# A recurrence of 64 steps: the transposition of the weights is moved from behind the state products to behind their sixth round of eight, in some of the steps

## The chip, the cores and the metric

The kernel runs on one core of a Trainium2 chip. The metric is the device time of one execution in microseconds (us). Before the change it was 16686.17 us, the median of three runs (16681.96 to 16693.16).

## The reference

The program is a whole audio tower of four layers. The change touches one part of it: the recurrent fast-weight layer in the third layer's attention, which is, for each of 64 positions `t` of a sequence and for all frames and heads (cut to what matters):

```python
def rec_step(carry, inp):
    R, h = carry
    zt, kt, vt, bt = inp
    qh = jax.nn.softmax(h, axis=-1)
    v_old = jnp.einsum('bhij,bhj->bhi', R, kt)
    R = R + (bt * (vt - v_old))[..., :, None] * kt[..., None, :]
    h = zt + jnp.einsum('bhij,bhj->bhi', R, qh)
    return ((R, h), h)
_, hs = jax.lax.scan(rec_step, (R0, h0), (z, rk, rv, rbeta))
```

An earlier stage of the kernel has already turned the updates of `R` into rows `ur`, so that `R` at step t is a sum of products of a row of `ur` and a key of `kr`. What is left for each step is `h = z + R softmax(h)`, for 246 independent states of 64 x 64 at a time. All is float32.

## The kernel before, in words

`recur_stage` runs eight passes (four pairs of heads, two halves of the frames), each of `SL = 64` steps. A pass keeps its states in two groups, a = 0 and a = 1, of 124 and 122 rows (frame and head on the partitions). The 64 steps are four quarters of `SC = 16` steps. The state matrices `R` hold what came before the current quarter; what came within the quarter is taken from its keys `K` and rows `U` directly. A step t with n = t mod 16 + 1 does, for a group:

- ScalarE: `e = exp(h - max)` with its sum (L2881).
- VectorE, `dots`: `pr = K * e` over n keys (L3000), its sum `dot` (L3005), then `w = dot * par8`, which spreads each dot over eight columns (L3009), then two small operations for the division by the sum. From t = 16 on, VectorE does `finish` of the other group between L3005 and L3009.
- TensorE, `turn`: transposes `w` into PSUM, as `wT` (L2921), one instruction.
- ScalarE, `spread`: copies `wT` to `W`, in the places that the next products read (L2868).
- TensorE, `turn_exp`: turns `e` into PSUM, as `eT` (L2927, two products, four MATMULs in the trace, since a float32 product is two). ScalarE, `spread_exp`, copies it to `E` (L2876, two copies). It serves the state products of the step's own `e`.
- TensorE, `state`: the product of `R` with `E`, eight rounds of four products of 32 columns each (L2939, 64 MATMULs), summed in the bank `acc[a]`.
- TensorE, `recent`: the product of `U` with `W` on top of it (L2948, 16 products, 32 MATMULs). Its last one tells VectorE.
- VectorE, `finish`: adds to the row of `H` (L3026 twice), and takes its maximum (L3027), which lets ScalarE do the next exp.

In the first quarter `R` is zero, and there are no state products. In the first three quarters the next quarter's state is prepared beside the steps: TensorE multiplies a sixteenth of it per step (`make_state`, L2964), ScalarE copies it to `made` (`take_state`, L2889), and GpSimd adds it to the old state, `R_new = made + R_old` (L2859, in the second and third quarter, 16 per quarter; in the first it copies, L2861).

There is no scheduler: each engine's order is written out by hand in its block, and the engines wait for each other by semaphores. The order of TensorE from step 16 on, which the change touches, is: state(0, t), turn(0, t), turn_exp(1, t), recent(0, t), make_state, state(1, t), turn(1, t), turn_exp(0, t + 1), recent(1, t). `turn` waits for `s_dot` (L3009 done), `recent` for `s_dg` (L2868 done). ScalarE's order from step 16 on is exp of group 1, spread(0, t), spread_exp(1, t), exp of group 0, spread(1, t), spread_exp(0, t + 1), take_state(t).

Of the kernel before, what the change touches and what calls it, by code (L numbers as in the profile page):

```python
# [441 lines left out]
SC = 8  # L442
# [2242 lines left out]
def recur_stage(nc, c, kr, ur, zz, hs):  # L2685


    SC, NL = 16, 4
# [5 lines left out]
    with Stage(nc, "recur") as st:  # L2694
# [91 lines left out]
        def run(i, half, following):  # L2786
            with st.step() as block:
# [128 lines left out]
                @block.tensor  # L2916
                def _(pe):
                    def turn(a, t):
                        n = t % SC + 1
                        pe.wait_ge(s_dot[a], t + 1)  # L2920
                        nc.tensor.transpose(wT[a][0:8 * n, 0:128], w[a][:, 0:n, :].rearrange("p s k -> p (s k)"), c.ident[:]).then_inc(s_tr[a], 1)  # L2921

                    def turn_exp(a, t):
                        cp = 2 * GROUPS[a][1]
                        pe.wait_ge(s_ex[a], t)
                        for h in range(2):
                            ins = nc.tensor.matmul(eT[a][64 * h:64 * h + 64, 0:128], e[a][0:cp, :], Ih[0:cp, h, :], start=True, stop=True)  # L2927
                        ins.then_inc(s_et[a], 1)

                    def state(a, t):  # L2930
                        rows = R[t // SC % 2][:].rearrange("p (a y) m d -> p a (y m) d", a=2)[:, a]
                        if t % SC == 0:
                            pe.wait_ge(s_rk, NMK * (t // SC))
                        pe.wait_ge(s_eg[a], 2 * (t - SC + 1))
                        for j in range(8):
                            u, v = divmod(j, 4)
                            for q in range(4):
                                m = 16 * q + 8 * u + v
                                nc.tensor.matmul(acc[a][32 * q:32 * q + 32, 0:2 * FD].rearrange("p (w d) -> p w d", w=2),  # L2939
                                                 E[a][:, EQ * q + 32 * j:EQ * q + 32 * j + 32], rows[:, m:m + 5:4, :], start=(j == 0), stop=False)  # L2940

                    def recent(a, t):
                        n = t % SC + 1
                        pe.wait_ge(s_dg[a], t + 1)
                        for j in range(4):
                            at = FD * (j % 2) if t >= SC else 0
                            for q in range(4):
                                ins = nc.tensor.matmul(acc[a][32 * q:32 * q + 32, at:at + FD], W[a][0:8 * n, 160 * q + 32 * j:160 * q + 32 * j + 32],  # L2948
                                                       U[a][0:8 * n, t // SC % 2, 4 * q + j, :], start=(t < SC and j == 0), stop=(j == 3))
                        ins.then_inc(s_sum[a], 1)  # L2950

                    def make_state(k, n):
                        b = NB * k + n // 4
                        pe.wait_ge(s_rin[b % 2], 16 * 12 * (b // 2 + 1))
                        if NMK * k + n:
                            pe.wait_ge(s_rc, 2 * (NMK * k + n))
                        a = n % 2
                        for x in range(4):
                            m = 4 * (n // 2) + x
                            for y in range(2):  # L2960
                                if 32 * y + m < GROUPS[a][1]:
                                    rows = slice(64 * a + 32 * y, 64 * a + 32 * y + SC)
                                    for h in range(2):
                                        ins = nc.tensor.matmul(Rp[y][64 * h:64 * h + 64, x, :], Ks[b % 2][rows, m % PB, h, :], Us[b % 2][rows, m % PB, h, :], start=True, stop=True)  # L2964
                        ins.then_inc(s_rm, 1)

                    for t in range(SL):
                        if t and t % SC == 0:
                            pe.wait_ge(s_in[t // SC], 16 * 24)
                        if t < SC:  # L2970
                            for a in range(2):
                                turn(a, t)
                                recent(a, t)
                                if t >= SC - NMK // 2:
                                    make_state(0, 2 * (t - (SC - NMK // 2)) + a)
                            if t == SC - 1:
                                turn_exp(0, SC)
                        else:
                            state(0, t)
                            turn(0, t)  # L2980
                            turn_exp(1, t)
                            recent(0, t)
                            if t < SL - SC:
                                make_state(t // SC, t % SC)
                            state(1, t)
                            turn(1, t)
                            if t + 1 < SL:
                                turn_exp(0, t + 1)
                            recent(1, t)
# [1237 lines left out]
```

## Time and profile before

| | |
|---|---|
| median of three runs | 16686.17 us |
| the profiled execution's own time | 16682.81 us |
| its span, from first to last instruction | 16681.0 us |
| granted clock of TensorE over the span | 0.824 of full |
| recurrence: from the first transposition of `w` to the last `finish` | from 9947.1 to 13578.8 us of the span |
| TensorE busy over the span | 12670.9 us (76%) |
| VectorE busy over the span | 9806.6 us (59%) |
| ScalarE busy over the span | 6771.4 us (41%) |
| state products, L2939, 49152 MATMULs | 1559.1 us busy |
| recent products, L2948, 32768 MATMULs | 785.7 us busy |
| transpositions of `w`, L2921, 1024 | 342.0 us busy |

TensorE's MATMULs are pipelined: their modelled ends reach past the start of the next ones, so a busy share near 100% doesn't mean that it has no pauses. Starts are what can be read. PE is TensorE's matmul, PEld its weight load, DVE VectorE, ACT ScalarE, POOL GpSimd. One step takes some 6 to 8 us, and there are 48 steps with state products in each of eight passes.

### The profile page before, as it was taken

What the parts mean: (1) busy time and instruction counts of PE and PEld (TensorE: products, weight loads), DVE (VectorE), ACT (ScalarE), POOL (GpSimd) and SP (SyncE); (2) the same over time, 40 slices, a digit from 0 to 9 for tenths busy, and PEclk for the clock granted to TensorE, in tenths of its full rate; (3) what the DMA queues carried; (4) which work ended last, traced back from release to release, by engine and by line L of the source; (5) the groups of instructions that cost most, each with busy time, mean ns of one, the idle gap of its engine ahead of it and who ended that gap; (6) DMA issues with size and microseconds to landing.
All of it is one profiled execution on the core that took longest, in us unless ns stands there. A gap on an engine that the chain in (4) does not pass through costs nothing. (4 is left out here: it accounts for less than half of the span.)

```text
span 16681.0 us, 559673 instructions
## 1 busy us (share of the span) xinstructions
PE 12670.9 (76%) x241781; PEld 9937.0 (60%) x241781; DVE 9806.6 (59%) x25450; ACT 6771.4 (41%) x17683; POOL 2665.7 (16%) x1778
## 2 busy tenths in 40 slices
PE   5605677886186498898999978988888885868887
PEld 4503475665154377777777757766666674745655
DVE  6561247776411566666666657777777755437885
ACT  3100125663021366666666643333333331336651
POOL 0028501000447011111111111111111100000001
PEclk9555558886586699999999988888888896968986
DMA  0412321003133211111111112122222244159862
GB/s 22 115 24 47 81 46 37 21 22 84 38 74 50 83 27 26 27 27 26 27 27 26 27 37 56 47 56 53 52 55 53 50 128 123 39 168 257 251 180 68
DMA packets 1829102, 1109.34 MB, mean 67 GB/s; under 512 B 1097198, under 2 KB 1751441, under 8 KB 1808657
## 3 DMA queue, kind: packets, MB, share of 16 engines
q1 hardware_dynamic: 1599239, 1015.52, 24.4%
q0 software_dynamic: 227328, 57.19, 2.4%
q8 instruction: 1936, 31.72, 0.8%
q14 instruction: 599, 4.91, 0.1%
HBM read 585.55 MB, written 484.53 MB: 64 GB/s over the span
## 5 line engine op out<-in xcount | busy, mean ns | idle before, releaser
L2939 PE MATMUL recur_acc<-recur_R,recur_E 128*32 128x128 f32 x49152 | 1559.1, 279 | 44.6 <-POOL recur_R L2859 27.8
L2939 PEld LDWEIGHTS recur_acc<-recur_R,recur_E 128*32 128x32 f32 x49152 | 1341.9, 112 | 107.3 <-issue 62.5
L2475 ACT ACTIVATE delta_B1l<-delta_pS 64x256 f32<-64x256 f32 x1968 | 743.6, 378 | 709.3 <-PE delta_pS L2375 683.6
L2475 ACT ACTIVATE delta_B0l<-delta_pS 64x256 f32<-64x256 f32 x1968 | 743.5, 378 | 623.4 <-PE delta_pS L2375 602.6
L3000 DVE TENSOR_TENSOR recur_pr<-recur_K,recur_e 124x64 f32<-124x64 f32 (+31 forms) x1024 | 751.1, 734 | 218.1 <-ACT recur_e L2881 171.8
L2510 POOL TENSOR_TENSOR delta_QK<-delta_QK,delta_mx 128x512 f32<-128x512 f32 x369 | 379.7, 1043 | 3044.4 <-DVE delta_mx L2563 3044.4
L2948 PE MATMUL recur_acc<-recur_U,recur_W 8*32 8x64 f32 (+1 forms) x32768 | 785.7, 244 | 105.2 <-ACT recur_W L2868 95.5
L2948 PEld LDWEIGHTS recur_acc<-recur_U,recur_W 8*32 8x32 f32 (+1 forms) x32768 | 596.9, 123 | 355.1 <-ACT recur_W L2868 346.9
L2868 ACT ACTIVATE recur_W<-recur_wT 8x128 f32<-8x128 f32 (+15 forms) x1024 | 278.1, 272 | 1277.1 <-PE recur_wT L2921 1260.3
L2881 ACT ACTIVATE recur_e<-recur_H,recur_mx 124x64 f32<-124x64 f32 x1008 | 350.8, 348 | 1056.9 <-DVE recur_mx L3027 1056.6
L3005 DVE TENSOR_REDUCE recur_dot<-recur_pr 124x1 f32<-124x64 f32 (+31 forms) x1024 | 736.8, 719 | 34.1
L3026 DVE SCALAR_TENSOR_TENSOR recur_H<-recur_acc,recur_rm,recur_H 124x64 f32<-124x64 f32 (+1 forms) x1536 | 435.8, 284 | 534.1 <-PE recur_acc L2948 493.8
L2375 PE MATMUL delta_pM<-delta_B1l 64*64 64x128 f32 (+1 forms) x11808 | 740.1, 256 | 5.3 <-ACT delta_B1l L2478 4.3
L2375 PE MATMUL delta_gp<-delta_W,delta_xc 128*128 128x512 f32 x1230 | 699.3, 653 | 37.2 <-DVE delta_xc L2546 37.0
L2375 PE MATMUL delta_pM<-delta_B0l 64*64 64x128 f32 (+1 forms) x11808 | 716.5, 255 | 4.8 <-ACT delta_B0l L2478 3.6
L2375 PE MATMUL delta_gp<-delta_KT 64*64 64x64 f32 x11808 | 563.0, 224 | 183.2 <-ACT delta_KT L2497 143.3
L2375 PEld LDWEIGHTS delta_pM<-delta_B1l 64*64 64x64 f32 x11808 | 600.2, 133 | 100.4 <-issue 89.1
L2375 PEld LDWEIGHTS delta_pM<-delta_B0l 64*64 64x64 f32 x11808 | 581.7, 133 | 126.0 <-ACT delta_B0l L2478 98.8
L1207 POOL DMA_INDIRECT hB<-experts_y,experts_idx x256 | 619.1, 2418 | 101.2 <-issue 80.8
L2525 DVE TENSOR_TENSOR delta_B1l<-delta_B1l,delta_pM 128x256 f32<-128x256 f32 x738 | 310.7, 421 | 545.1 <-PE delta_pS L2375 545.1
L2921 PE MATMUL recur_wT<-const_ident,recur_w 128*8 128x128 f32 (+15 forms) x1024 | 342.0, 334 | 374.3 <-DVE recur_w L3009 368.6
L2375 PE MATMUL delta_pM<-delta_B 64*64 64x128 f32 x7872 | 536.7, 275 | 101.4 <-issue 86.4
(626 smaller groups left out, 34033.6 us busy)
## 6 DMA issues: line engine op xcount, KB each, us to landing
scr<-rel_BD SPq DMA_DIRECT2D x128, 1288.0 KB
rel_sc<-scr SPq DMA_DIRECT2D x128, 861.0 KB
xnT<-ln_xT SPq DMA_DIRECT2D x64, 492.0 KB, 3.0
kr<-delta_QK SPq DMA_DIRECT2D x492, 64.0 KB, 2.3
ur<-delta_Uf SPq DMA_DIRECT2D x492, 64.0 KB, 2.2
zz<-delta_Z SPq DMA_DIRECT2D x492, 64.0 KB, 2.2
recur_K<-kr SPq DMA_DIRECT2D x64, 448.0 KB
recur_H<-zz SPq DMA_DIRECT2D x64, 448.0 KB
```

The lines of the kernel that those rows point to most:

```text
L1207: nc.gpsimd.indirect_dma_start(acc[:, :], bass.IndirectOffsetOnAxis(ap=idx[:, e, 4 * q + t:4 * q + t + 1], axis=0), y[n % 3][:, t, :], Non ...
L2375: return nc.tensor.matmul(o, l, r, start=True, stop=True)
L2475: ins = nc.scalar.activation(new[h, :, 0, :], pS[k][HALF[1 - x], 0:4, :], ACT.Copy)
L2510: nc.gpsimd.tensor_tensor(third(j), third(j), mx[:, rows_of(j)].unsqueeze(2).to_broadcast([128, FH, FD]), ALU.subtract).then_inc(s_sh, 1)
L2525: V.tensor_tensor(level(k, G % 2, l + 1)[:, :, 2, :], u, pM[k][:, :, 1, :], ALU.subtract if l == 0 else ALU.add).then_inc(s_dv[k], 1)
L2881: nc.scalar.activation(e[a][0:cp], Hh[a][0:cp, t, :], ACT.Exp, bias=mx[a][0:cp, 0:1], accum_out=rs[a][0:cp, 0:1]).then_inc(s_ex[a], 1)
L2921: nc.tensor.transpose(wT[a][0:8 * n, 0:128], w[a][:, 0:n, :].rearrange("p s k -> p (s k)"), c.ident[:]).then_inc(s_tr[a], 1)
L2939: nc.tensor.matmul(acc[a][32 * q:32 * q + 32, 0:2 * FD].rearrange("p (w d) -> p w d", w=2), E[a][:, EQ * q + 32 * j:EQ * q + 32 * j + 32], ...
L2948: ins = nc.tensor.matmul(acc[a][32 * q:32 * q + 32, at:at + FD], W[a][0:8 * n, 160 * q + 32 * j:160 * q + 32 * j + 32], U[a][0:8 * n, t // ...
L3000: V.tensor_tensor(pr[0:cp, 0:n, :], K[a][0:cp, r0:r0 + n, :], e[a][0:cp, None, :].to_broadcast([cp, n, FD]), ALU.mult).then_inc(s_own[a], 1)
L3005: own[a](V.tensor_reduce(dot[a][0:cp, 0:n], pr[0:cp, 0:n, :], AX.X, ALU.add))
L3026: own[a](V.scalar_tensor_tensor(row, acc[a][0:cp, FD * z:FD * z + FD], rm[a][0:cp, z:z + 1], row, ALU.mult, ALU.add))
```

## The change

In the first eight steps of a quarter (t mod 16 < 8), `turn(a, t)` is issued inside `state(a, t)`, behind its sixth round. In the other steps it is issued right behind the state products, as before. The first quarter has no state products, and its order is as it was.

```diff
                     def state(a, t):
+                        soon = t % SC < 8
                         rows = R[t // SC % 2][:].rearrange("p (a y) m d -> p a (y m) d", a=2)[:, a]
                         if t % SC == 0:
                             pe.wait_ge(s_rk, NMK * (t // SC))
                         pe.wait_ge(s_eg[a], 2 * (t - SC + 1))
                         for j in range(8):
+                            if soon and j == 6:
+                                turn(a, t)
                             u, v = divmod(j, 4)
                             for q in range(4):
                                 m = 16 * q + 8 * u + v
                                 nc.tensor.matmul(acc[a][32 * q:32 * q + 32, 0:2 * FD].rearrange("p (w d) -> p w d", w=2),
                                                  E[a][:, EQ * q + 32 * j:EQ * q + 32 * j + 32], rows[:, m:m + 5:4, :], start=(j == 0), stop=False)
+                        if not soon:
+                            turn(a, t)
...
                         else:
                             state(0, t)
-                            turn(0, t)
                             turn_exp(1, t)
                             recent(0, t)
                             if t < SL - SC:
                                 make_state(t // SC, t % SC)
                             state(1, t)
-                            turn(1, t)
                             if t + 1 < SL:
                                 turn_exp(0, t + 1)
                             recent(1, t)
```

So 8 steps x 3 quarters x 8 passes x 2 groups = 384 of the 768 transpositions behind state products move. No instruction is added or taken away, and the orders of VectorE, ScalarE, GpSimd and the DMA queue stay as they were.

TensorE in the second quarter, steps 17 and 18 of a pass, before (each row is a run of equal instructions: `recur_acc<-recur_R` are the state products, `recur_wT` the moved transposition, `recur_eT` the turned exp, `recur_acc<-recur_U` the recent products, `recur_Rp` the next state):

```order
L2939 MATMUL recur_acc<-recur_R,recur_E 32x128 x32
L2921 MATMUL recur_wT<-const_ident,recur_w 16x128
L2927 MATMUL recur_eT<-recur_Ih,recur_e 64x128 x2
L2948 MATMUL recur_acc<-recur_U,recur_W 32x64 x16
L2964 MATMUL recur_Rp<-recur_Us,recur_Ks 64x64 x16
L2939 MATMUL recur_acc<-recur_R,recur_E 32x128 x32
L2921 MATMUL recur_wT<-const_ident,recur_w 16x128
L2927 MATMUL recur_eT<-recur_Ih,recur_e 64x128 x2
L2948 MATMUL recur_acc<-recur_U,recur_W 32x64 x16
```

The same place with the change:

```order
L2942 MATMUL recur_acc<-recur_R,recur_E 32x128 x24
L2921 MATMUL recur_wT<-const_ident,recur_w 16x128
L2942 MATMUL recur_acc<-recur_R,recur_E 32x128 x8
L2927 MATMUL recur_eT<-recur_Ih,recur_e 64x128 x2
L2953 MATMUL recur_acc<-recur_U,recur_W 32x64 x16
L2969 MATMUL recur_Rp<-recur_Us,recur_Ks 64x64 x16
L2942 MATMUL recur_acc<-recur_R,recur_E 32x128 x24
L2921 MATMUL recur_wT<-const_ident,recur_w 16x128
L2942 MATMUL recur_acc<-recur_R,recur_E 32x128 x8
L2927 MATMUL recur_eT<-recur_Ih,recur_e 64x128 x2
L2953 MATMUL recur_acc<-recur_U,recur_W 32x64 x16
```

The transposition now stands eight products (16 MATMULs) earlier, and the turned exp follows the last two rounds in its place.

## Rows read from the trace of the kernel before

**Rows 1.** Who waited for whom, whole recurrence: us in total, times, longest.
```profile
PEld recur_acc L2948 <- ACT recur_W L2868: 346.9, 1024, 0.7
...
PEld recur_acc L2939 <- issue: 62.5, 63, 2.0
```
**Rows 2.** Timeline of TensorE, second quarter, step 20: start us, us, instruction, xcount.
```profile
10533.98 1.95 PE L2939 MATMUL recur_acc<-recur_R,recur_E 128*32 128x128 f32 x64
10535.86 0.29 PE L2921 MATMUL recur_wT<-const_ident,recur_w 128*40 128x128 f32 x1
...
10536.51 0.65 PE L2948 MATMUL recur_acc<-recur_U,recur_W 40*32 40x64 f32 x32
...
10537.71 1.95 PE L2939 MATMUL recur_acc<-recur_R,recur_E 128*32 128x128 f32 x64
10539.60 0.29 PE L2921 MATMUL recur_wT<-const_ident,recur_w 128*40 128x128 f32 x1
10539.82 0.44 PE L2927 MATMUL recur_eT<-recur_Ih,recur_e 124*64 124x128 f32 x4
...
10540.83 0.86 PE L2939 MATMUL recur_acc<-recur_R,recur_E 128*32 128x128 f32 x24
```
**Rows 3.** TensorE's weight loads, same step; in brackets idle time before, and its releaser.
```profile
10536.51 0.49 PEld L2948 LDWEIGHTS recur_acc<-recur_U,recur_W 40*32 40x32 f32 x32 [0.23 <-ACT recur_W L2868]
...
10539.60 0.10 PEld L2921 LDWEIGHTS recur_wT<-const_ident,recur_w 128*40 128x40 f32 x1 [0.20 <-issue]
```
**Rows 4.** Timeline of the other engines, same step.
```profile
10534.43 1.28 POOL L2859 TENSOR_TENSOR recur_R<-recur_made,recur_R 128x512 f32<-128x512 f32 x1 [6.16 <-ACT recur_made L2889]
...
10534.94 0.82 DVE L3009 TENSOR_TENSOR recur_w<-recur_dot,recur_par 124x40 f32<-124x40 f32 x1
...
10540.52 0.67 ACT L2889 ACTIVATE recur_made<-recur_Rp 128x256 f32<-128x256 f32 x2
...
10541.27 1.28 POOL L2859 TENSOR_TENSOR recur_R<-recur_made,recur_R 128x512 f32<-128x512 f32 x1 [5.56 <-ACT recur_made L2889]
```
**Rows 5.** Timeline of TensorE, fourth quarter, step 50, group 0.
```profile
10751.41 1.96 PE L2939 MATMUL recur_acc<-recur_R,recur_E 128*32 128x128 f32 x64
10753.30 0.28 PE L2921 MATMUL recur_wT<-const_ident,recur_w 128*24 128x128 f32 x1
10753.51 0.44 PE L2927 MATMUL recur_eT<-recur_Ih,recur_e 122*64 122x128 f32 x4
10753.93 0.65 PE L2948 MATMUL recur_acc<-recur_U,recur_W 24*32 24x64 f32 x32
10754.51 1.95 PE L2939 MATMUL recur_acc<-recur_R,recur_E 128*32 128x128 f32 x64
```
**Rows 6.** Timeline of VectorE, the same half-step.
```profile
10752.38 0.17 DVE L3009 TENSOR_TENSOR recur_w<-recur_dot,recur_par 124x24 f32<-124x24 f32 x1
```
**Rows 7.** Groups of instructions by form, recurrence: count, busy us, mean ns, idle before.
```profile
L2859 POOL TENSOR_TENSOR recur_R<-recur_made,recur_R 128x512 f32<-128x512 f32 x256 | 327.6, 1280 | 1578.1 <-ACT recur_made L2889 1578.1
```
**Rows 8.** Timeline of TensorE, fourth quarter, steps 57 and 59.
```profile
10794.33 0.65 PE L2948 MATMUL recur_acc<-recur_U,recur_W 72*32 72x64 f32 x32
10794.80 1.93 PE L2939 MATMUL recur_acc<-recur_R,recur_E 128*32 128x128 f32 x64
...
10809.43 0.44 PE L2927 MATMUL recur_eT<-recur_Ih,recur_e 122*64 122x128 f32 x4
10809.80 0.66 PE L2948 MATMUL recur_acc<-recur_U,recur_W 96*32 96x64 f32 x32
```
**Rows 9.** Timeline of TensorE in a later stage: transpositions, then products of the same shape.
```profile
13604.75 0.58 PE L3115 MATMUL dout_tp<-const_ident,dout_t 123*128 123x123 f32 x4
13605.18 1.04 PE L3124 MATMUL dout_yp<-dout_wo,dout_tT 128*123 128x128 f32 x8
```
**Rows 10.** Timeline of TensorE, third quarter, step 33 of the fourth pass.
```profile
11539.32 0.49 PE L2948 MATMUL recur_acc<-recur_U,recur_W 16*32 16x64 f32 x18 [1.45 <-issue]
```
**Rows 11.** Busy us (x count) of PE, PEld, DVE, ACT, POOL; granted clock; DMA share, GB/s.
```profile
11551.79:11556.37 4.58, 4.58 (x103) 3.55 (x101) 0.45 (x1) 0.73 (x4) 0.00 (x0) 0.63 0.26 63
```

## The prediction

> **What bounds the kernel now.** I read four views, for the recurrence alone, since nothing outside it changes. First the waits: they say what TensorE stands for. The largest that the change aims at is the recent products' wait for ScalarE's copy of the transposed weights, 346.9 us over 1024 times [rows 1]. Then the timelines of one step in the second quarter [rows 2 to 4] and one in the fourth [rows 5, 6], because the step, not the total, tells what a wait is worth. All offsets below are counted from the start of a state product, S.
>
> In step 50 nothing interrupts TensorE: S, transposition at 1.89, turned exp at 2.10, recent products at 2.52, next S at 3.10 [rows 5]. TensorE bounds these steps; VectorE's multiply by `par8`, which the transposition needs, runs from 0.97 to 1.14 and is long ready [rows 5, 6]. In step 20, group 1, the times are the same: 1.89 to the transposition, 2.11 to the turned exp, 3.12 to the next S [rows 2]. Group 0 has `make_state` behind it, 3.73 to the next S, and one difference that the TensorE rows don't show: its multiply starts at 0.96 and lasts 0.82 instead of 0.17, to 1.78. GpSimd's addition runs from 0.45 to 1.73, and the multiply ends 0.05 after it [rows 4, 6]. I read this as the multiply being held by the addition. Today that costs nothing: at 1.78 TensorE is just through with the state products, and the transposition comes at 1.88 [rows 2].
>
> The reader is also to see the pauses around the transposition. The weight load before it idles 0.20 with "issue" as its releaser, so it waits for nobody [rows 3]. It is a change of shape: state products (32 columns, four side by side), transposition (whole columns), turned exp (64 columns). Two checks: recent products of 24 rows take 0.58 to the next S, those of 72 rows 0.47 [rows 5, 8], although both are followed by the same semaphore wait, so the 0.11 goes with the shape and not with the wait; and four transpositions followed by products of like shape take 0.43, that is 0.107 each, with no pause [rows 9].
>
> **The change, part by part.** The eight rounds take 1.89 - 0.20 = 1.69 up to the pause [rows 3, 5], 0.21 each; at a steady pace, with 0.107 to 0.109 for 128 columns [rows 9] and two passes a round, 0.22. Two rounds are 0.44.
>
> Moved, a free half-step. The transposition comes at 1.89 - 0.44 = 1.45. Its multiply must be ready by then: 1.14 in the fourth quarter, and earlier in group 1 of the middle quarters. So it doesn't wait. From it to the seventh round I take 0.205, as from the transposition to the turned exp today (0.21 [rows 5]); nearest below is 0.107 [rows 9], without a change of shape. The seventh round starts at 1.655, its last MATMUL 0.375 later (16 MATMULs are four groups 0.109 apart, and a start after a pause costs 0.025 once) at 2.03, and the turned exp 0.205 behind it at 2.24, against 2.10: later by **0.14**. The split adds one more change of shape.
>
> Removed: the wait for ScalarE's copy. The copy now ends well before. The turned exp to recent products can shrink from 0.43 to 0.37, its value in step 59 [rows 8], for its own four MATMULs and a change of shape remain. So recent products start at 2.61 against 2.52, and a free half-step gets longer by **0.08**. Bounds: with 0.107 out of the transposition it is -0.02; with no gain at the recent products +0.14. I take the middle value, since the rows show this very pair of shapes in the other order [rows 3, 5].
>
> Moved, a held half-step: group 0 where the addition runs. GpSimd's addition follows ScalarE's copy of `made`, which stands behind the two copies of the turned exp. It starts 10541.27 - 10539.82 = 1.45 after group 1's turned exp [rows 2, 4]. From there to the next S it is now 1.01, and then 0.37 + 0.44 + 0.14 = 0.95. So the addition starts at 0.50 and ends at 1.78, the multiply ends at 1.84, and the transposition starts at 1.90, where TensorE wanted it at 1.45: **TensorE stands 0.45**, with two state rounds, the other group's turned exp and the recent products queued behind it. Then 2.10 seventh round, 2.48 its last, 2.69 turned exp, 3.06 recent products, against 2.53: longer by **0.53**. Today the same lateness lies under rounds seven and eight. VectorE behind it has room: what it does between the held multiply and its next `finish` is short at up to eight keys; if that cover were gone, the lateness would be added once more, which I price at nothing.
>
> Counts. Additions: 256, 32 per pass, 16 in each middle quarter [rows 7]. The addition of step t holds the multiply of step t + 1, so of the first eight steps of those two quarters seven are held, 14 per pass, 112 in all (the eighth begins a quarter, where S waits for the addition before). Free are 384 - 112 = 272.
>
> Sum: 112 x 0.53 = 59, 272 x 0.08 = 22, together 81. Cover: TensorE also stands for "issue" in the middle of uniform runs, 1.45 us in one of them [rows 10], 62.5 us over 63 times before state products alone [rows 1]. No data is late there; I read it as late instructions. Where such a stall falls before round seven the hold is over, and a slower TensorE asks for its instructions a little later; I take off 4, about an eighth of the part of these stalls that could lie in the first halves. So **+77 us**. The profiled execution's own time, 16682.81, lies 3.4 below the median, 16686.17; from the median it is 16763.
>
> **A rule of the Trainium skill against the rows.** The load of the transposition's weights idles 0.20 behind the last state MATMUL while its operand is ready [rows 3]. The Trainium skill, "TensorE: Matmul & The Clock Gate", Part 2 and Part 3, says that TensorE's queue pulls weight loads ahead of running MATMULs when their row groups don't conflict or when they go to the background weights. By that a transposition could slip between two rounds with no pause. The trace doesn't agree for this pair of shapes. What the sum would be without the pauses is rival 1.
>
> **Rivals.**
> 1. *The split costs no pause.* Transposition 0.107 after round six and round seven 0.107 after it. For it: the transpositions that need no pause [rows 9]. Against: the idle load [rows 3]. A free half-step: 1.35 transposition, 1.46, 1.81 last MATMUL, 2.02 turned exp, 2.39 recent: -0.13, together -35; a held one still waits to 1.90, 2.01, 2.36, 2.57, 2.94: +0.41, together +46. Sum +11: 16697, no change. 6%.
> 2. *Faster: no pause, and no hold.* One mechanism, that of rival 1, in all 384 places: it needs the addition out of the way. ScalarE's copy of the weights of group 1 comes 0.44 earlier, and if that, not the turned exp, sets when `made` is copied, the addition ends before 1.40. Price -0.13 x 384 = -50: 16636. It decides when the addition ends before 1.40. Against it: the copies of the turned exp stand between and need TensorE. 5%.
> 3. *The cover is larger.* If late instructions hide half of the sum: +40, 16726. 12%.
> 4. *The clock falls as well.* A state product at granted clock 0.63 took 4.58 for its half-step instead of 3.1 [rows 11], so 1.5 more. TensorE now stands 0.45 in seven successive steps. Against: even behind a stop of 1.45 the next products ran at full pace [rows 10]. One fall per middle quarter is 16 x 1.5 = +24: 16787; one in each held step would be 112 x 1.5 = +168: 16931. 7%.
>
> **How the numbers follow.** My forecast, hold and pause both there, has 70%: 16763, between 16725 (pauses at their low bound, 43) and 16795 (no gain at the recent products, 38 + 66 = 104). About 0.2%, 33 us, is what a measurement can tell from no change. Slower than 16719: the forecast 69%, rival 3 9% (its low side falls within), rival 4 7%: 0.85. Within: rival 1 5% and what is left of the forecast and rival 3: 0.09. Faster: 0.06, rival 2 and a rest. The range of 8 in 10 takes in rival 3, the bounds, and one fall of the clock per quarter: 16712 to 16805.
>
> **What would show it.** In the profile after: in free half-steps, state MATMULs in two runs, 48 and 16, with pauses of 0.20 on both sides of the transposition, turned exp at 2.24, recent products at 2.61, next S at 3.18. The recent products' wait for ScalarE gone in 384 of 1024 places. In held ones the transposition at 1.90 with an idle TensorE before it and VectorE's `recur_w` as its releaser, next S at 4.26. It would be wrong if the seventh round followed the transposition by 0.11, or if the multiply ended before 1.45 in group 0 of steps 17 to 23.

## The result, and the profile after

The changed kernel took 16729.48 us, median of 19 runs (16701.87 to 16752.46); the kernel before, beside it, 16685.37 us (19 runs, 16662.25 to 16703.78). The ratio is 1.0026, with a 95% interval of 1.0020 to 1.0032: **slower by 44 us**, 33 to 53. The forecast was +77 us, 16763, with a range of 16712 to 16805. The sign and the mechanisms held; the measured cost is 33 us smaller than the forecast.

The profiled execution has a span of 16724.3 us, 43.3 more than before. All of it lies in the recurrence: its eight passes take 3541.2 us before and 3584.4 after, each counted from its first transposition of `w` to its last recent product, +43.2.

TensorE in step 20 of the second pass, as in [rows 2] (columns as there):

```profile
10541.61 1.52 PE L2942 MATMUL recur_acc<-recur_R,recur_E 128*32 128x128 f32 x48
10543.50 0.29 PE L2921 MATMUL recur_wT<-const_ident,recur_w 128*40 128x128 f32 x1 [0.38 <-DVE recur_w L3012]
10543.72 0.64 PE L2942 MATMUL recur_acc<-recur_R,recur_E 128*32 128x128 f32 x16
10544.30 0.44 PE L2927 MATMUL recur_eT<-recur_Ih,recur_e 122*64 122x128 f32 x4
10544.67 0.65 PE L2953 MATMUL recur_acc<-recur_U,recur_W 40*32 40x64 f32 x32
...
10545.87 1.52 PE L2942 MATMUL recur_acc<-recur_R,recur_E 128*32 128x128 f32 x48
10547.32 0.29 PE L2921 MATMUL recur_wT<-const_ident,recur_w 128*40 128x128 f32 x1
10547.54 0.64 PE L2942 MATMUL recur_acc<-recur_R,recur_E 128*32 128x128 f32 x16
10548.11 0.44 PE L2927 MATMUL recur_eT<-recur_Ih,recur_e 124*64 124x128 f32 x4
10548.48 0.65 PE L2953 MATMUL recur_acc<-recur_U,recur_W 40*32 40x64 f32 x32
10549.06 0.64 PE L2942 MATMUL recur_acc<-recur_R,recur_E 128*32 128x128 f32 x16
```

Group 1, the free half-step, reads 1.45 to the transposition, 2.24 to the turned exp, 2.61 to the recent products and 3.19 to the next state product, where the prediction had 1.45, 2.24, 2.61 and 3.18. Group 0, the held one, reads 1.89, 2.69, 3.06 and 4.26, where it had 1.90, 2.69, 3.06 and 4.26. The weight loads of group 0's half-step, and GpSimd's and VectorE's rows of it, as in [rows 3, 4]:

```profile
10543.50 0.10 PEld L2921 LDWEIGHTS recur_wT<-const_ident,recur_w 128*40 128x40 f32 x1 [0.64 <-DVE recur_w L3012]
...
10544.30 0.20 PEld L2927 LDWEIGHTS recur_eT<-recur_Ih,recur_e 122*64 122x64 f32 x4 [0.20 <-issue]
10544.66 0.49 PEld L2953 LDWEIGHTS recur_acc<-recur_U,recur_W 40*32 40x32 f32 x32 [0.17 <-issue]
```
```profile
10542.12 1.28 POOL L2859 TENSOR_TENSOR recur_R<-recur_made,recur_R 128x512 f32<-128x512 f32 x1 [6.15 <-ACT recur_made L2889]
```
```profile
10542.58 0.87 DVE L3012 TENSOR_TENSOR recur_w<-recur_dot,recur_par 124x40 f32<-124x40 f32 x1
```

The load before the recent products no longer names ScalarE's copy, as it did in [rows 3]: what is left there, 0.17, is the change of shape. The load before the transposition now idles 0.64 for the multiply, which ends 0.05 behind GpSimd's addition. The waits of the whole recurrence, as in [rows 1]:

```profile
PEld recur_acc L2953 <- ACT recur_W L2868: 256.5, 640, 0.7
...
PEld recur_acc L2942 <- issue: 58.9, 75, 2.0
```

640 places are left of 1024, so the wait for the copy went in exactly the 384 that moved, and 90 us of waiting with it. The kernel is slower all the same, because 384 new pauses and 112 held transpositions stand in their place.

The steps cost what the sum said. Their medians give 0.53 to 0.54 for a held half-step and 0.08 for a free one, so 112 x 0.535 + 272 x 0.08 = 82 us. The passes got only 43 longer. So 39 us of the cost are hidden somewhere, where the prediction took off 4 (39 us is 82 - 43). The experiments ask two things: whether the two terms are what they were taken for, and what hides 39 us.

### The profile page after: what moved, and what is told of

Read it like the earlier page. It is cut to its first block and busy times, and to the rows that moved or that the text cites. A ratio compares the mean times of both kernels' runs of the same rounds, so it can differ in the third digit from the quotient of the medians.

```text
span 16724.3 us, 559673 instructions
## 1 busy us (share of the span) xinstructions
PE 12682.6 (76%) x241781; PEld 9898.1 (59%) x241781; DVE 9824.3 (59%) x25450; ACT 6778.9 (41%) x17683; POOL 2668.4 (16%) x1778
## 5 line engine op out<-in xcount | busy, mean ns | idle before, releaser
L2942 PE MATMUL recur_acc<-recur_R,recur_E 128*32 128x128 f32 x49152 | 1623.6, 279 | 40.8 <-POOL recur_R L2859 27.9
L2942 PEld LDWEIGHTS recur_acc<-recur_R,recur_E 128*32 128x32 f32 x49152 | 1304.9, 111 | 147.4 <-issue 58.9
```

## Experiments: the terms of the sum

Theory: the pauses and the hold cost what the steps show, and what hides part of it are TensorE's stalls for late instructions, with the clock falls behind them (a fall: a stretch in which the granted clock is 0.5 of full, the level of 1.2 GHz). Rivals: the hold is the whole cost; or both terms are too large by the same factor. The kernel before, measured beside these four, took 16662.85 us (30 runs).

**Only the free places.**

```diff
-                        soon = t % SC < 8
+                        soon = t % SC < 8 and (a == 1 or t % SC == 0 or t >= SL - SC)
```

> The transposition moves only where GpSimd's addition doesn't hold the multiply: group 1 in the first eight steps of a quarter, both groups in step 0 of a quarter and in the fourth quarter, 272 places. Theory (the step times of the prediction are right, and what was missing of its sum was stalls for late instructions and falls of the clock, which shrink only where TensorE is held back long): +0.08 us each, +22 us in all, stalls in the second and third quarter as before. Rival 1 (the pauses around the transposition cost nothing in sum, the whole +44 comes from the hold): 0 us. Rival 2 (both parts of the sum are too large by the same factor, 44/81): +12 us.

Measured: 16679.78 us, ratio 1.0008 (0.9999 to 1.0017), +13 us with an interval of -2 to +28. The time alone excludes neither +22 nor +12, nor quite 0. The steps decide against the rival that the pauses are free: behind the first step of a quarter, the moved half-steps at full clock read 3.18 to 3.20 in place of 3.10 to 3.13.

**Only the held places.**

```diff
-                        soon = t % SC < 8
+                        soon = 0 < t % SC < 8 and a == 0 and t < SL - SC
```

> The transposition moves only in the 112 held places: group 0, steps 1 to 7 of the second and third quarter. Theory: the seven half-steps get 0.53 us longer each, 59 us in all, and the stalls for late instructions with the clock falls behind them give back some 35: +24 us. Rival 1 (the whole cost is the hold): +44 us. Rival 2 (same factor): +32 us. The half-step of group 0 should read 4.26 in place of 3.73 in all three, so the difference lies in what is idle for late instructions and in the granted clock.

Measured: 16705.15 us, ratio 1.0026 (1.0015 to 1.0036), +43 us, 25 to 60. The expected half-step of 4.26 was a slip of mine: group 1 keeps its old order here, so the addition starts at 0.45 and not at 0.50, and the half-step reads 4.21.

```profile
10536.69 1.52 PE L2942 MATMUL recur_acc<-recur_R,recur_E 128*32 128x128 f32 x48
10538.53 0.29 PE L2921 MATMUL recur_wT<-const_ident,recur_w 128*40 128x128 f32 x1 [0.32 <-DVE recur_w L3012]
...
10540.90 0.32 PE L2942 MATMUL recur_acc<-recur_R,recur_E 128*32 128x128 f32 x4
```

That is +0.47, 52 us over 112. The time is that of the first rival, and the theory's +24 lies just outside the interval. The rival's reason, free pauses, is refuted by the steps of the run above; what the time does show is that the hold is most of the cost, and that I set the cover too high for this kernel: 52 by the steps against 43.

**Behind the seventh round.**

```diff
-                            if soon and j == 6:
+                            if soon and j == 7:
```

> As the change, but the transposition stands behind the seventh round in all 384 places. Free places: the same three changes of shape, +0.08 each, the transposition at 1.67 in place of 1.45, next S still 3.18. Held places: the multiply still ends at 1.84, one state round less is queued behind it: next S at 4.05 in place of 4.26, +0.31 each. Sum of the steps 22 + 35 = 57 against 81 for the change; theory with a cover of some 25 to 35: +25 us, rival (the hold is all, the pauses nothing): 112 x 0.23 = +26 us with the free places at 3.10. The profile tells the two apart, not the time.

Measured: 16696.54 us, ratio 1.0024 (1.0015 to 1.0033), +40 us, 25 to 55. In the profile the free half-steps read 3.18, the held ones 4.05:

```profile
10516.86 1.74 PE L2942 MATMUL recur_acc<-recur_R,recur_E 128*32 128x128 f32 x56
10518.76 0.29 PE L2921 MATMUL recur_wT<-const_ident,recur_w 128*40 128x128 f32 x1 [0.16 <-DVE recur_w L3012]
...
10520.91 0.32 PE L2942 MATMUL recur_acc<-recur_R,recur_E 128*32 128x128 f32 x4
```

Both are the theory's numbers. The transposition is no later than behind round six, 1.90, but one round less is queued behind it. The time is less good for the theory: it said +25, after a cover of 25 to 35 us, and +40 is more, though still within the interval. By the steps alone it would be +57.

**The hold taken away.** ScalarE's copy of the next state goes ahead of its exp of group 0, so that GpSimd adds in group 1's half-step:

```diff
                             spread_exp(1, t)
+                            if t < SL - SC:
+                                take_state(t)
                             if t + 1 < SL:
                                 exped(0, t)
...
-                        if SC <= t < SL - SC:
-                            take_state(t)
```

> The changed kernel, with ScalarE's copy of the next state moved ahead of its exp of group 0, in place of behind the copies of the turned exp. GpSimd's addition then runs in group 1's half-step, before the multiply of group 0 is due. Theory (the multiply is held by the addition): the multiply of group 0 in steps 1 to 7 lasts 0.17 to 0.2 us again and the half-step 3.81 in place of 4.26, all 384 places are free: +31 us from the step times, little cover, and perhaps some 10 us less since steps 8 to 13 no longer wait for it either. Rival (the multiply is late for another reason, and only ends with the addition by chance): it still ends at 1.84, and the time is that of the change, +44 us.

Measured: 16677.97 us, ratio 1.0009 (1.0000 to 1.0018), +15 us. The multiply lasts 0.19 again, and the transposition comes at 1.45 in group 0 as well:

```profile
10518.55 1.52 PE L2942 MATMUL recur_acc<-recur_R,recur_E 128*32 128x128 f32 x48
10519.51 0.19 DVE L3012 TENSOR_TENSOR recur_w<-recur_dot,recur_par 124x40 f32<-124x40 f32 x1
...
10520.00 0.29 PE L2921 MATMUL recur_wT<-const_ident,recur_w 128*40 128x128 f32 x1
```

So the addition does hold the multiply. The Trainium skill, "SBUF — State Buffer", section "SBUF: two separate sides", says that a VectorE operation with two operands in SBUF and a GpSimd operation that reads SBUF exclude each other for a whole instruction; by that rule, the trace agrees, with 0.87 against 0.19. The time is below the +31 of the steps, and two things that were not in the sum went into it. The addition is now done when a quarter begins, so that the wait of 1.74 us for it before the first state product of the third and the fourth quarter (16 times, 27.9 us in the changed kernel) is gone. And the hold has moved: my hope for steps 8 to 13 failed, the second halves of the quarters take 1387.9 us in all, against 1347.6 in the changed kernel. In the trace of step 28 the addition holds the multiply of group 1:

```profile
10579.84 1.27 POOL L2859 TENSOR_TENSOR recur_R<-recur_made,recur_R 128x512 f32<-128x512 f32 x1 [6.26 <-ACT recur_made L2889]
...
10580.25 0.98 DVE L3012 TENSOR_TENSOR recur_w<-recur_dot,recur_par 122x104 f32<-122x104 f32 x1
```

From the eleventh key on this multiply lasts 0.62 to 1.23 in place of 0.24 to 0.28, and in steps 10 to 14 group 1's half-step takes 3.46 to 3.49 in place of 3.03 to 3.05. Up to ten keys it is group 0's `pr` that is held instead (1.54 in place of 0.69 at eight keys), and there it costs TensorE nothing. So the +15 is not a clean price of the pauses, but the length of the multiply and the transposition at 1.45 decide what the run was made for.

## Experiments: what hides half of the cost

**The same two kernels once more.** The kernel before, measured beside these, the late loads and the 72 rows below, took 16685.19 us (21 runs).

> The kernel before, unchanged, for a second profile of its recurrence. Theory (stalls for late instructions and falls of the clock in the recurrence are a property of the kernel, some 100 us, of which the change hides some 30): the stall and clock time above the step times is again 90 to 120 us. Rival (it is chance): it lies where that of the changed kernel lay, 60 to 90 us.

> The changed kernel, unchanged, on the chip of this call, for the same question. Theory: the recurrence's step times are again 73 us longer in sum than before, and stall and clock time is about 80 us, 20 to 40 less than before; the time +44 us, between +30 and +55. Rival (the hidden part is chance): stall and clock time as before, and +65 to +80 us.

Measured: the kernel before 16679.55 us in its one run; the changed one 16734.18 us, ratio 1.0025 (1.0015 to 1.0035). The eight passes take 3525.8 and 3573.1 us, +47.3. Above the shortest instance of each half-step the recurrence has 94 us of stalls and slow clock in the kernel before (108 in the first profile), and 66 in the changed one (79). So each pair has 29 or 30 us less. The times agree that something is hidden again, with +42 by the ratio (49 by the medians) where the steps have 82. How the hidden part is made up is less firm: the two profiles of one kernel already differ by 13 or 14 us in this sum.

The sum can be taken apart with the profiles' clock records and the stops, by which I mean idle times of TensorE of over 0.6 us with "issue" as the releaser. Slow clock is counted as half of the time at 0.5, in steps 16 to 63, which is a little more than it costs: a fall of 3.4 us makes a half-step of 3.2 last 4.7.

```
us over eight passes        slow clock     stops
kernel before, 1st profile       76         22.5
changed, 1st profile             59         11.9
kernel before, 2nd profile       58         20.2
changed, 2nd profile             41         13.6
```

The change goes with 17 us less slow clock in both pairs, and with 11 and 7 us less in stops. All of the slow clock lies in the first four steps of a quarter. In the first pair its difference isn't behind stops at all: it is a stretch of slow clock that comes from the first quarter, before the first state product, and reaches into the second, 49 us before and 31 after. In most passes it ends 5.5 to 8 us behind the quarter's start, in four of eight passes before and in one after only at 12 or 18.5 (2 and 1 in the second pair), and no stop stands ahead of it. The first 20 us of the second quarter, second pass, before and after (the third number from the end is the granted clock):

```profile
10496.29:10516.29 20.00, 19.15 (x389) 14.88 (x385) 5.48 (x26) 4.59 (x22) 2.28 (x3) 0.54 0.29 75
```
```profile
10504.64:10524.64 20.00, 17.36 (x447) 13.44 (x443) 7.62 (x33) 5.04 (x24) 2.29 (x3) 0.76 0.33 80
```

Whether the change ends this stretch sooner, or one profile of each kernel differs by chance, is not shown.

Where it is hidden shows by steps. The table gives the changed kernel minus the one before, in us over eight passes, by sums of starts read from the traces; "by the steps" is 0.61 or 0.16 per step times eight:

```
steps of a quarter     by the steps   first pair   second pair
0 to 3, quarter 2          16            -2             5
0 to 3, quarter 3          16            -3            10
0 to 3, quarter 4           5            11            -4
4 to 7, all three          44            37            40
```

From the fifth step on the cost arrives nearly whole. In the first four, of 37 us only 6 and 11 arrive. There the stops lie, mostly in the middle of runs of equal products: 17 in each profile of the kernel before, 10 and 12 in the changed kernel, every one in step 1 or 3 of a quarter. In the first step of the second quarter the clock also comes back to full at another point, and that step is 10 us shorter in sum in the first pair, 3 in the second.

**Where the stops come from.** Steps 1 and 3 are those behind which the next quarter's keys and start rows are loaded. The loads three steps later each:

```diff
-                        for s in range(1, 13):
+                        for s in range(1, 16):
                             sp.wait_ge(s_mx[0], k * SC + s)
-                            if nxt:
-                                if k == NL - 1 and s == 3:
-                                    sp.wait_ge(s_out, 16 * 2 * 16)
+                            if nxt and k == NL - 1 and s == 3:
+                                sp.wait_ge(s_out, 16 * 2 * 16)
+                            if nxt and s >= 4:
...
-                            if k and s >= 5:
+                            if k and 5 <= s <= 12:
```

> The kernel before, with the loads of the next quarter's keys, start rows and values issued three steps later each (steps 4 to 15 of a quarter in place of 1 to 12). Theory (TensorE stalls for late instructions because their fetches lie behind these transfers in the DMA engines, early in a quarter, and the clock falls behind a stall): stalls in steps 1 to 3 of a quarter shrink, those that move to steps 4 to 15 lie partly under waits for VectorE: -10 to -50 us. Rival (the stalls come from the rows of the next state or from the fetches themselves): 0 us, and the stalls stay in steps 1 to 3.

Measured: 16731.31 us, ratio 1.0030 (1.0018 to 1.0041), **+46 us, where 10 to 50 less were expected**. The stops moved exactly as the theory says: none of over 0.6 us is left in steps 1 to 3, 20 lie in step 4 and 12 in step 6, three later. But they got more and longer, 48.8 us in all. One of them, and the waits of the recurrence:

```profile
10085.84 2.08 PE L2939 MATMUL recur_acc<-recur_R,recur_E 128*32 128x128 f32 x33 [2.10 <-issue]
```
```profile
PEld recur_acc L2939 <- issue: 81.0, 71, 2.5
...
PE recur_acc L2939 <- issue: 29.5, 26, 2.2
```

Before, the second of these rows has 9.6 us in 12 times. The slow clock rose with them, to 82 us from 58 in the profile of the kernel before beside it. Why the same loads delay more at steps 4 to 6 (the rows of the next state and the stores start there too) wasn't separated. That it is instructions that are late is read from the DMA packets of the first profile: packets of 16 KB in the instruction queue start 3.9 us apart in the middle case, and 6.65 us lie between the last two ahead of the stop of [rows 10] (11530.10 and 11536.75). Ahead of all 17 stops this distance is 4.5 to 7.0 us. No run changed the instruction packets themselves, so late instructions remain the reading, not a thing shown.

**Keys and start rows at the end of a quarter.** Values at steps 1 to 8, keys at 12 and 13, start rows at 14 and 15:

```diff
-                                    if s <= 2:
-                                        load_keys(sp, *nxt, a, HALVES[s - 1])
-                                    elif s <= 4:
-                                        load_start(sp, *nxt, a, HALVES[s - 3])
-                                    else:
-                                        load_values(sp, *nxt, a, *divmod(s - 5, 2))
+                                    if s <= 8:
+                                        load_values(sp, *nxt, a, *divmod(s - 1, 2))
+                                    elif 12 <= s <= 13:
+                                        load_keys(sp, *nxt, a, HALVES[s - 12])
+                                    elif s >= 14:
+                                        load_start(sp, *nxt, a, HALVES[s - 14])
```

> The kernel before, with the order of a quarter's loads changed: the values at steps 1 to 8, the keys at 12 and 13, the start rows at 14 and 15 (before: keys 1 and 2, start rows 3 and 4, values 5 to 12). When keys and start rows were issued three steps later, the stalls moved by three steps with them. Theory (a transfer of keys or start rows delays TensorE's instructions, and a fall of the clock may follow): the stalls of steps 1 to 3 go, those at 12 to 15 lie under waits for VectorE; stall and clock time of 94 to 108 us in the recurrence falls to 30 to 60: -30 to -70 us. Rival (any transfer does it, or VectorE's steps don't hide it): 0 to -15 us.

Measured: 16665.96 us against 16685.72 us (25 runs), ratio 0.9987 (0.9978 to 0.9995), -20 us (-37 to -8), between the rival's -15 and the theory's -30. No stop is left in steps 1 to 11, and the first halves of the quarters take 1371.9 us in place of 1425.0 and 1405.8. The stops went to steps 12 and 14, 21 of them with 26.4 us, and the second halves take 1385.0 in place of 1348.8 and 1352.3. The waits for VectorE don't hide them, as I had hoped: above the shortest instance of each half-step stand 116 us, where 30 to 60 were expected. At a quarter's first step the profile shows 11 more idle times with "issue" as the releaser, but each is 1.73 us long and they aren't new. They are the wait for the last addition, which stood there 16 times before (27.8 us) and of which the row now names only five:

```profile
PE recur_acc L2939 <- POOL recur_R L2859: 8.7, 5, 1.7
```

So the order of loads moves the stops and doesn't remove them. Why the kernel is 20 us faster all the same isn't shown: its passes take 3524.5 us in the profile, the kernel before's 3541.2 in the first and 3525.8 in the second.

**The change on top of that.** This is the test of the theory: the first four steps now have no such stops to hide anything.

> The changed kernel with the same order of loads. Theory (the change's step times cost 82 us, and 35 to 39 of them were hidden in both pairs of profiles by stalls and clock falls in the first steps of a quarter): with few stalls left there is little to hide it, so this is 65 to 80 us slower than the kernel before with the same order of loads. Rival (what is hidden is not these stalls): again 44 us slower than that one.

Measured: 16731.74 us, ratio 1.0027 (1.0016 to 1.0038); against the kernel with the same order of loads 1.0027 / 0.9987 = 1.0040, **+66 us** in place of +44. Steps 0 to 3 of the three quarters now cost 20, 16 and 1 us more, together 37, which is the 37 by the steps. The first halves are 1442.8 - 1371.9 = 71 us longer, against 44 and 50 without the new order of loads. In these two profiles the passes differ by 3602.3 - 3524.5 = 78 us. Resampled from the runs on record, the medians of the two kernels lie 56 to 72 us apart, and this difference is 4 to 33 us larger than with the loads in their old place. So less is hidden here, as the theory says. But the test doesn't separate the stops from the slow clock: that is 59 us without the change and 75 with it, 16 more where the other two pairs have 17 less, and 7 us of it lie in the first four steps, so that the 37 of the table is met in part by luck. What hides the rest, between 66 and 82, was not traced.

## Experiments: the pause and the shape

**Recent products over 72 rows.** Does the pause before the next state product go with the wait or with the number of rows? Here the order of TensorE is that of the kernel before.

> The kernel before, with the order of before, but the recent products of the first eight steps of a quarter are taken over 72 rows of the weights in place of 8 to 64: nine keys are turned and copied at least, those not yet reached are zero. Theory (a pause comes with a change of shape, not with a wait): the pause of 0.14 before the next state product becomes the 0.03 of step 57, 0.11 less in each of 384 half-steps, -42 us; the transposition of 72 columns in place of 8 to 64 delays what follows by 0.01 to 0.02, +6; a memset more on VectorE at a quarter's first step, under 0.2 each, +0 to +5. Sum -33, less some 10 that stalls for late instructions take back: -20 to -35 us. Rival (the pause is the semaphore wait's, and the 0.47 of step 57 has another reason): 0 to +10 us, half-steps of 3.11 as before.

```diff
                     def turn(a, t):
-                        n = t % SC + 1
+                        n = max(t % SC + 1, 9)
...
                     def recent(a, t):
-                        n = t % SC + 1
+                        n = max(t % SC + 1, 9)
...
+                        if t % SC == 0:
+                            own[a](V.memset(w[a][0:cp, 1:9, :], 0.0))
```

Measured: 16673.02 us against 16685.19 us, ratio 0.9993 (0.9984 to 1.0002), -12 us, less than expected and not clear of none. The pause did what the theory says. In step 50 the next state product comes 0.47 behind the recent ones, at 3.02 in place of 3.10:

```profile
10755.20 1.95 PE L2939 MATMUL recur_acc<-recur_R,recur_E 128*32 128x128 f32 x64
...
10757.75 0.65 PE L2948 MATMUL recur_acc<-recur_U,recur_W 72*32 72x64 f32 x32
10758.22 0.29 PE L2939 MATMUL recur_acc<-recur_R,recur_E 128*32 128x128 f32 x4
```

The same wait stands between them, only the rows differ, 72 for 24: it is the shape. The expectation failed elsewhere: in the middle quarters group 0's half-step got longer by what group 1's got shorter, 3.72 to 3.80 against 3.10 to 3.02. The state product starts earlier, the addition and with it the multiply don't. That is the hold again, in a kernel whose order of TensorE is that of before.

**Both together**, the 72 rows and the keys and start rows at the end of a quarter:

> The kernel before with this order of loads and with the recent products over 72 rows. Theory: half-steps of the fourth quarter get 0.09 to 0.10 shorter each, those of the middle quarters 0.08 shorter in group 1 and 0.08 longer in group 0, as measured: -13 us against the same order of loads alone, so -45 to -85 us against the kernel before, which would be the fastest of all. Rival: as for the order of loads, 0 to -28 us.

Measured: 16664.77 us, ratio 0.9990 (0.9982 to 0.9999), -17 us where 45 to 85 less were expected. Its passes are 10 us shorter in the profile, 3514.1 against 3524.5, but in time it can't be told from the order of loads alone, 16665.96. Both are faster than the kernel before, by some 20 us.

## Why the prediction was right in sign, and where its size was off

- **What bounds a step, and the free half-step: right.** TensorE's own order sets it. One more change of shape, 0.14 to the turned exp, 0.06 back at the recent products, 0.08 in sum.
- **The held half-step: right.** 1.90 against 1.89, 4.26 against 4.26. That the multiply was held, and didn't end with the addition by chance, was an inference; the kernel with the early copy shows it.
- **The counts: right.** 384 waits for the copy gone, 112 held, and the sum of the steps 81 against 82 measured.
- **The cover: this step failed.** "I take off 4, about an eighth of the part of these stalls that could lie in the first halves." It was 39 in the first pair and 35 in the second. I had spread the stalls evenly over the recurrence, and had counted no slow clock into the cover. Each stop of over 0.6 us lies in step 1 or 3 of a quarter and all slow clock in the first four steps, so inside the eight steps that the change slows. The profiles after have 11 and 7 us less in stops and 17 us less slow clock, and from the fifth step on the cost arrives nearly whole. Why these two shrink, and how much of it is the change's doing, stays open in part: with the loads elsewhere the cost rose to 66 us, but the slow clock rose too. Rival 3 had the size, with half of the sum hidden and 16726; measured 16729.48. I gave it 12%, and it named late instructions alone. The measured time also lies inside the bounds of my own forecast, 16725 to 16795, but that is luck: the low bound stands for cheap pauses, and the pauses had their full price.
- **The rivals of a free split and of a faster kernel fell** with the pauses on both sides of the transposition, 0.20 before it and 0.22 from its start to the seventh round's. The weight load waits there although its operand is ready, as [rows 3] already showed. Rival 4, an added fall of the clock, didn't come: the granted clock is 0.825 over the span after, 0.824 before.
- **A slip in the bounds.** The upper one, "no gain at the recent products, 38 + 66 = 104", gives 16790, or 16786 with the 4 taken off, and not 16795. It changes no verdict.

## What to carry to other kernels

An instruction of another shape, moved from the end of a uniform run of matmuls into it, adds one change of shape, and saves at most the wait that it was moved for: here 0.14 against 0.06. A step that is moved ahead must be weighed against the latest moment of its operand, which here wasn't VectorE's work but GpSimd's addition that it stands behind. And a cost worked out from clean steps can come out twice too large, as here, where the same steps also hold stalls and slow clock: find out in which steps those lie before setting the cover. A stop that a profile puts down to "issue" has to be compared with the waits that stand in the same place in the other kernels, by its length.

## What was not expected of the hardware

- TensorE stops for 0.6 to 3.4 us, with no data late, in the steps in which the large loads of keys and of start rows are issued (112 rows each), and the stops follow when the loads are moved: from steps 1 and 3 to 4 and 6, or to 12 and 14.
- A GpSimd addition of 1.28 us held VectorE's small multiply from 0.19 to 0.87, and when it was moved, VectorE's `pr` from 0.69 to 1.54. In the profile this is no wait: it is part of VectorE's own duration.
- A slow clock from a quarter without state products reached 5.5 to 18.5 us into the next, at different lengths in passes of one and the same kernel.
- At a change of shape the weight loads idle 0.17 to 0.20 us, and rows count as well as columns: 64 rows or fewer before a product of 128 rows cost 0.11, which 72 rows don't (0.58 to 0.47) though the columns are the same.
